# Third attention: the chain of its first half in quarters of 128 columns, with the PSUM banks dealt anew

## The chip, the core and the metric

The kernel runs on one core of a Trainium2 chip. A core has the tensor engine (PE, with its weight loads PEld), the vector engine (DVE), the scalar engine (ACT), GpSimd (POOL) and SyncE (SP), which here starts transfers. Each engine works off its own instructions in the order in which the program gives them, and waits only on semaphores. The metric is the device time of one execution in microseconds. The kernel before takes 116.27 us, the median of 3 runs (115.99 to 117.38).

## What is computed

A small vision tower on 16 images, each of 64 tokens with 64 features: patch embedding with layer norm, a windowed attention with two feed-forward nets, a second attention with a periodic bias, and a last block of a causal attention with 4 heads and a mixture of 8 gated experts, 2 of them for each token. The change lies in the last block, between its attention and its experts:

```python
x = h                                    # 1024 tokens x 64 features
q, k, v = rope(heads(rmsnorm(x)))        # 4 query heads, 2 key and value heads
scores = where(causal, q @ k.T / sqrt(16), -1e30)
y = softmax(scores) @ v                  # the third attention
x = x + y @ wo.T
flat = rmsnorm(x)                        # x * rsqrt(mean(x*x) + 1e-6) * ln2_w
probs = softmax(flat @ router_w.T)       # two best experts, weights that sum to 1
hh[e] = silu(flat @ w1[e].T) * (flat @ w3[e].T)
out = sum over e of weights[:, e] * (hh[e] @ w2[e].T)
result = layernorm(h + x + out)
```

## The kernel before

All activations lie in tiles of 128 partitions and 512 columns (COLS = 512). With tokens on the partitions, 512 columns are 8 blocks of 64 features. HC = 256 columns are one half (g = 0 or 1, four blocks), P = 128 columns a quarter (two blocks). PS is the PSUM, 8 banks of 512 columns of float32. The kernel writes the order of each engine out by hand and joins engines with named semaphores, so a step is late if anything ahead of it on its own engine is late. The tables of banks (TURNED_BANKS, UP_BANKS) say where products land.

The third attention works in four steps i = 0 to 3, two for each half g (i = 2g, 2g+1). For each step DVE takes the row maximum and subtracts it (shift3, L1217 and L1219), PE transposes (turn3, L589), ACT takes the exponential (probabilities3, L918), and PE multiplies by the values (mix3, L603). When both steps of a half are mixed, its chain follows:

- DVE divides by the row sum (divide: reciprocal L1228, product L1230),
- PE transposes back (mixed_to_features, L411), ACT copies out (attended_copy3, L922),
- PE opens a bank with the residual h4 in two float32r parts (open3, L613, which waits for POOL's split L1080 and L1082) and adds the output projection to it (output3, L618),
- ACT squares (squares3, L926), DVE sums (sum_squares3, L1392), POOL takes the power -0.5 (L1087),
- DVE scales the result twice, once rounded to float32r and once in full (high_part L1398, normalised L1374), and takes the difference (low_part, L1380),
- PE transposes both parts (parts_to_features, L626), and DVE and ACT copy one part each (turned_copy, L1385 and L937).

Then the expert products can begin: 22 chunks n = 0 to 21, the first 11 on half 0 and the others on half 1. A chunk is four float32r products of 512 columns on PE (L690, L691), a Silu on ACT (L956) and a product on DVE (L1437). The chain of half 1 runs between the first seven chunks: its output projection stands at n = 1, its transposes at n = 6. Its division and its transposes back (L411 again, bank 7) stand before chunk 0. stay_awake (L306) issues products of zeros that nobody reads.

On PE the order around the change is turn3(2), mixed_to_features(0), open3(0), output3(0), turn3(3), mix3(2), open3(1), mix3(3), stay_awake, parts_to_features(0), mixed_to_features(1), chunk 0. On DVE it is shift3(2), two scalings to h4 (L1168), divide(0), shift3(3), sum_squares3(0), high_part(0), normalised(0), low_part(0), divide(1), turned_copy(0), residual(0) (L1388), chunk 0.

Of the kernel before, what the change touches and what calls it, by code (L numbers as in the profile page):

```python
# [86 lines left out]
def build(nc, x0, x1, pack_a, pack_b, pack_c, pack_d, pack_e, out):  # L87
    with ExitStack() as ctx:
# [157 lines left out]

        def vo_part(h2, p, g):

            return vo[HALF * h2:HALF * h2 + HALF, p, 4 * g:4 * g + 4, :, h2, 0:HD]
# [47 lines left out]
        def _(pe):  # L297
# [109 lines left out]
            def mixed_to_features(name, bank, g):  # L407

                pe.wait_ge(sem(name + "_divided"), g + 1)
# [49 lines left out]
            mixed_to_features("att1", 0, 0)  # L459
# [12 lines left out]
            mixed_to_features("att1", 1, 1)  # L472
# [135 lines left out]
            def open3(g):  # L608


                pe.wait_ge(sem("h4_split"), 2 * (g + 1))
                for n in range(2):
                    mm(PS[:, 4 * g, 0:HC], ident_r[:, :], xf[:, g, n], start=(n == 0), stop=(n == 1), skip_group_check=True)  # L613

            def output3(g):
                pe.wait_ge(sem("att3_ready"), g + 1)
                for u in (2 * g, 2 * g + 1):
                    t = mm(PS[:, 4 * g, (u % 2) * P:(u % 2 + 1) * P], attended3[:, u * P:(u + 1) * P], c("fo"),  # L618
                           start=False, stop=True, skip_group_check=True)
                t.then_inc(sem("fo_mm"), 1)  # L620

            def parts_to_features(g):
                pe.wait_ge(sem("parts_ready"), g + 1)
                for s in range(2):
                    for u in (2 * g, 2 * g + 1):
                        t = tp(PS[:, TURNED_BANKS[s][g], (u % 2) * P:(u % 2 + 1) * P], parts[:, 2 * u + s].rearrange("q l d -> q (l d)"), ident)  # L626
# [37 lines left out]
            def half_ready(g):  # L664
                pe.wait_ge(sem("xf_ready0"), g + 1)
                pe.wait_ge(sem("xf_ready1"), g + 1)

            pe.wait_ge(sem("up_split"), 2)
            half_ready(0)
            for n in range(2 * CH):  # L670
                g, ch = n // CH, n % CH
                if n == 1:
                    output3(1)
                if n == 2:
                    pe.wait_ge(sem("h45_ready"), 1)
                if n == PARTS_AT:
                    pe.wait_ge(sem("h45_ready"), 2)
                    parts_to_features(1)
                if n == ROUTE_AT:
                    half_ready(1)  # L680
# [91 lines left out]
        def _(act):  # L772
# [147 lines left out]
            def attended_copy3(g):  # L920
                act.wait_ge(sem("att3_back"), g + 1)
                f(half(attended3, g), PS[:, 3 + 4 * g, 0:HC], ACT.Copy).then_inc(sem("att3_ready"), 1)  # L922

            def squares3(g):
                act.wait_ge(sem("fo_mm"), g + 1)
                f(squares_eps[:, 4 * g:4 * g + 4, 0:D], PS[:, 4 * g, 0:HC].rearrange("q (t d) -> q t d", d=D), ACT.Square,  # L926
                  scale=float(D) ** -0.5).then_inc(sem("rms2_squared"), 1)

            def high_part(g):

                act.wait_ge(sem("rms2_normed"), g + 1)
                f(parts[:, 4 * g:4 * g + 4, 0, :].bitcast(F32R), tiles(h5n)[:, 4 * g:4 * g + 4], ACT.Copy)\
                    .then_inc(sem("high_ready"), 1)

            def turned_copy(g):
                act.wait_ge(sem("parts_turned"), g + 1)
# [724 lines left out]
```

## Time and profile before

| | before |
|---|---|
| median of 3 runs | 116.27 us (115.99 to 117.38) |
| the profiled execution, its own time | 116.27 us |
| its span in the trace | 114.5 us |
| mean granted clock of the tensor engine | 0.989 |

```profile
span 114.5 us, 2195 instructions
...
PE 100.3 (88%) x825; PEld 65.2 (57%) x828; DVE 81.4 (71%) x173; ACT 64.0 (56%) x125; POOL 33.2 (29%) x68
...
PE   5998986899999998977699888899999999999720
...
DVE  0001515688979899889588984579589999986981
ACT  5003556776623853937378658467476667478040
POOL 7500017841840000000532083030012350869100
PEclk9999999999999999999999999999999999999995
...
PE 65%; DVE 20%; ACT 8%; issue 3%; POOL 1%; ACTq 0%; DVEq 0%; POOLq 0%
```

The first line is the span; the second gives busy time, share and instructions of each engine. The next five cut the span into 40 slices of 2.9 us, each digit the busy share in tenths, and PEclk the granted clock in tenths. The last line is the chain of work that ended last, shared out by engine. The third attention and its chain take slices 21 to 25, the expert products begin in the 26th. In the timeline below a row is start, duration, engine, line, operation, output<-inputs, and how often; a pair of brackets holds the idle time before it and who ended it. Rows of one kind that follow each other are merged, and their duration is then from the first start to the last end.

### The profile page before, as it was taken

The numbers are of one execution on the slowest core, as the hardware profiler recorded it, in microseconds if no ns is written. First come the engines' busy times: TensorE is split into PE (matmuls) and PEld (weight loads), VectorE is DVE, ScalarE is ACT, GpSimd is POOL, SyncE is SP. The second block draws the span as 40 slices with busy tenths as digits, with TensorE's granted clock in tenths as the row PEclk, the third lists the DMA queues.
The fourth block names the chain that finished last, engine by engine and source line by source line (L and its number), as shares of the span: only waits on it lengthen the run. The fifth ranks groups of instructions, "written<-read, shape, count | busy, mean of one in ns | idle before, by whom it ended". The sixth has DMA issues, their size and how long they took to land.

```text
span 114.5 us, 2195 instructions
## 1 busy us (share of the span) xinstructions
PE 100.3 (88%) x825; PEld 65.2 (57%) x828; DVE 81.4 (71%) x173; ACT 64.0 (56%) x125; POOL 33.2 (29%) x68
## 2 busy tenths in 40 slices
PE   5998986899999998977699888899999999999720
PEld 2344545567766765564378665687887884334400
DVE  0001515688979899889588984579589999986981
ACT  5003556776623853937378658467476667478040
POOL 7500017841840000000532083030012350869100
PEclk9999999999999999999999999999999999999995
DMA  3999993000000000000000000000000000000004
GB/s 109 399 397 416 445 407 136 0 0 0 0 6 0 0 3 6 3 0 0 0 0 6 0 0 6 0 0 0 0 0 6 3 0 0 3 0 0 0 0 92
DMA packets 2682, 6.99 MB, mean 61 GB/s; under 512 B 1264, under 2 KB 1392, under 8 KB 2544
## 3 DMA queue, kind: packets, MB, share of 16 engines
q1 hardware_dynamic: 2128, 6.72, 15.0%
q10 hardware_dynamic: 544, 0.13, 0.5%
q8 instruction: 6, 0.10, 0.4%
q14 instruction: 4, 0.03, 0.1%
HBM read 6.59 MB, written 0.26 MB: 60 GB/s over the span
## 4 chain that ended last, share of the span: by engine, by line
PE 65%; DVE 20%; ACT 8%; issue 3%; POOL 1%; ACTq 0%; DVEq 0%; POOLq 0%
PE PS L690 9%; PE PS L691 9%; PE PS L698 7%; PE PS L314 4%; PE PS L339 4%; PE PS L558 3%; PE PS L378 3%; PE PS L306 3%; PE PS L389 3%; ACT shared_f L791 3%; PE PS L349 3%; PE PS L403 3%; DVE shifted L1219 2%; DVE top L1217 2%; DVE sq_sums L1157 1%
## 5 line engine op out<-in xcount | busy, mean ns | idle before, releaser
L690 PE MATMUL PS<-xf,up_hi 128*128 128x512 f32 x44 | 17.8, 405 | 0.2 <-DVE xf L1385 0.2
L1437 DVE TENSOR_TENSOR shared_h<-PS,shared_f 128x512 f32<-128x512 f32 x22 | 15.0, 683 | 3.4 <-ACT shared_f L956 3.1
L691 PE MATMUL PS<-xf,up_lo 128*128 128x512 f32 x44 | 17.3, 394 | 0.0
L956 ACT ACTIVATE shared_f<-PS 128x512 f32<-128x512 f32 x22 | 13.1, 596 | 6.4 <-PE PS L691 6.2
L777 ACT ACT_TABLE_LOAD x9 | 11.5, 1283 | 0.9 <-PEq L1652 0.7
L1217 DVE TENSOR_REDUCE top<-PS 128x8 f32<-128x512 f32 x12 | 8.3, 688 | 2.5 <-PE PS L378 2.2
L690 PEld LDWEIGHTS PS<-xf,up_hi 128*128 128x128 f32 x44 | 8.3, 188 | 2.2 <-issue 0.4
L691 PEld LDWEIGHTS PS<-xf,up_lo 128*128 128x128 f32 x44 | 8.3, 188 | 1.8
L1219 DVE TENSOR_TENSOR shifted<-PS,top 128x512 f32<-128x512 f32 x12 | 8.3, 692 | 0.4
L852 ACT ACTIVATE probs<-PS 128x512 f32<-128x512 f32 x8 | 4.8, 597 | 5.9 <-PE PS L389 5.8
L791 ACT ACTIVATE shared_f<-PS,pack_b_sb 128x512 f32<-128x512 f32 x8 | 5.2, 684 | 4.9 <-PE PS L339 4.9
L698 PE MATMUL PS<-shared_h,down_w 128*64 128x512 f32 x32 | 7.7, 605 | 0.0
L314 PE MATMUL PS<-shared_x 128*64 128x256 f32 x48 | 7.1, 431 | 0.0
L1071 POOL TENSOR_SCALAR std<-sq_sums 128x8 f32<-128x8 f32 x1 | 0.2, 202 | 22.6 <-DVE sq_sums L1157 22.6
L306 PE MATMUL PS<-idle_bf 128*128 128x512 bf16 (+1 forms) x14 | 5.3, 492 | 1.5 <-POOL idle_bf L999 1.3
L1513 DVE TENSOR_TENSOR shared_x<-PS,up_w 128x512 f32<-128x512 f32 x8 | 5.2, 686 | 1.5 <-PE PS L698 1.1
L349 PE MATMUL PS<-shared_f,pack_b_sb 128*64 128x256 f32 x32 | 5.0, 405 | 1.0 <-ACT shared_f L791 0.9
L1235 DVE TENSOR_SCALAR pos_b<-pack_a_sb 128x64 f32<-128x64 f32 x1 | 0.3, 254 | 7.8 <-DMA pack_a_sb<-pack_a_dram 7.8
L1157 DVE TENSOR_REDUCE sq_sums<-squares 128x4 f32<-128x256 f32 x6 | 2.5, 418 | 4.6 <-ACT squares L800 4.4
L982 ACT ACTIVATE up_w<-PS 128x512 f32<-128x512 f32 x8 | 4.2, 599 | 2.7 <-PE PS L712 2.7
L378 PE MATMUL PS<-shared_h,q_groups 64*128 64x256 f32 x32 | 5.5, 422 | 0.0
L1125 POOL TENSOR_TENSOR shared_x<-shared_x 128x512 f32<-128x512 f32 x4 | 5.1, 1280 | 1.4 <-DVE shared_x L1513 1.3
(206 smaller groups left out, 210.1 us busy)
## 6 DMA issues: line engine op xcount, KB each, us to landing
shared_x<-x_dram SPq DMA_DIRECT2D x3, 576.0 KB, 4.6
shared_x<-x_dram SPq DMA_DIRECT2D x3, 512.0 KB, 7.2
up_w<-pack_d_dram SPq DMA_DIRECT2D x1, 1408.0 KB, 11.5
pack_c_sb<-pack_c_dram SPq DMA_DIRECT2D x1, 796.5 KB, 13.0
pack_b_sb<-pack_b_dram SPq DMA_DIRECT2D x1, 455.0 KB, 8.6
down_w<-pack_e_dram SPq DMA_DIRECT2D x1, 352.0 KB, 13.4
pack_a_sb<-pack_a_dram SPq DMA_DIRECT2D x1, 162.0 KB, 5.7
out_dram<-normed SPq DMA_DIRECT2D x2, 64.0 KB, 1.7
```

The costliest lines, as they stand in the source:

```text
L306: mm(PS[:, bank, 0:cols], idle_bf[:, 0:P], idle_bf[:, 0:cols], start=True, stop=True)
L314: m = mm(PS[HALF * s:HALF * s + HALF, 4 + g, 0:HC], x0_sb[:, n, PAIR + k * D:PAIR + (k + 1) * D], piece[:, n, (2 * k + s) * HC:(2 * k + s ...
L378: t = mm(PS[:, SCORE_BANKS[w % 2] + s, 0:HC], q_groups[r, w ^ s].rearrange("q h n -> q (h n)"), k_slots[r, w ^ s].rearrange("q h n -> q (h ...
L690: mm(up, up_hi[:, at:at + P], moving, start=True, stop=False)
L691: mm(up, up_lo[:, at:at + P], moving, start=False, stop=True).then_inc(sem("up_mm"), 1)
L698: t = mm(PS[HALF * s:HALF * s + HALF, bank, tok], down_w[:, DOWN_AT[ch]:DOWN_AT[ch] + D], hh[:, ch, s, tok], start=True, stop=True)
L777: f(table_use[:, :], const(1.0), func)
L791: f(hidden[:, m, :, g * HC:(g + 1) * HC], PS[:, u_banks[g]:u_banks[g] + 2, m * HC:(m + 1) * HC], ACT.Gelu_apprx_tanh, bias=b("ff1_b")[:, m ...
L956: f(gate[:, n % UPBUF, :], PS[:, UP_BANKS[n % UPBUF][0], :], ACT.Silu).then_inc(sem("gated"), 1)
L1217: v.reduce_max(tops, rows, AX).then_inc(sem(name + "_top"), 1)
L1219: v.tensor_tensor(shifted[:, n % 2, :].rearrange("q (b h n) -> q b h n", b=2, n=N), rows, tops.unsqueeze(3).to_broadcast([P, 2, 4, N]), AL ...
L1437: v.tensor_tensor(hh[:, ch, :, g * HC:(g + 1) * HC], PS[:, UP_BANKS[n % UPBUF][1], :].rearrange("q (s c) -> q s c", s=2), gate[:, n % UPBU ...
```

## The change

Half 0's chain, from the division to the copies, is done in two quarters u = 0, 1 of 128 columns, each in banks of its own; half 1 stays whole. Besides:

- The openings of the residual stand ahead of the transposes back. Quarter 0 is turned back into bank 4 and quarter 1 into bank 3 (BACK_BANKS); they are opened in banks 0 and 1 (H5_BANKS).
- shift3(3) is taken apart: its maximum stays behind the division, its subtraction stands behind both sums of squares.
- The transposes of the parts of quarter 0 stand ahead of mix3(3), those of quarter 1 behind it (banks 3, 2 and 5, 6, PARTS_BANKS). stay_awake is gone.
- All four copies of the transposed parts of half 0 are DVE's, and divide of half 1 stands behind them.
- ACT does both quarters' copies and squares ahead of probabilities3(2).
- POOL takes three powers, two of 128x2 and one of 128x4, in place of two of 128x4.

```diff
-        TURNED_BANKS = ((1, 4), (3, 7))
+        TURNED_BANKS = (4, 7)
+        BACK_BANKS = (4, 3)
+        H5_BANKS = (0, 1)
+        PARTS_BANKS = ((3, 2), (5, 6))
...
+            def quarter_to_features(u):
+                pe.wait_ge(sem("att3_divided"), u + 1)
+                tp(PS[:, BACK_BANKS[u], 0:P], quarter(s2, u), ident).then_inc(sem("att3_back"), 1)
...
+            def open3_quarters():
+                pe.wait_ge(sem("h4_split"), 2)
+                for u in range(2):
+                    for n in range(2):
+                        mm(PS[:, H5_BANKS[u], 0:P], ident_r[:, :], xf[:, 0, n, u * P:(u + 1) * P], start=(n == 0), stop=(n == 1), skip_group_check=True)
+
+            def output3_quarter(u):
+                pe.wait_ge(sem("att3_ready"), u + 1)
+                mm(PS[:, H5_BANKS[u], 0:P], quarter(attended3, u), c("fo"), start=False, stop=True, skip_group_check=True)\
+                    .then_inc(sem("fo_mm"), 1)
+
+            def quarter_parts_to_features(u):
+                pe.wait_ge(sem("parts_ready"), u + 1)
+                for s in range(2):
+                    t = tp(PS[:, PARTS_BANKS[u][s], 0:P], parts[:, 2 * u + s].rearrange("q l d -> q (l d)"), ident)
+                t.then_inc(sem("parts_turned"), 1)
...
             turn3(2)
-            mixed_to_features("att3", 3, 0)
-            open3(0)
-            output3(0)
+            open3_quarters()
+            quarter_to_features(0)
+            quarter_to_features(1)
+            output3_quarter(0)
+            output3_quarter(1)
             turn3(3)
             mix3(2)
-            open3(1)
+            open3_last()
+            quarter_parts_to_features(0)
             mix3(3)
-            stay_awake(2, 1)
-            parts_to_features(0)
-            mixed_to_features("att3", 7, 1)
+            quarter_parts_to_features(1)
+            mixed_to_features("att3", 7, 1, 3)
...
-            half_ready(0)
+            pe.wait_ge(sem("xf_ready0"), 4)
...
             values3(1)
+            attended_quarter(0)
+            attended_quarter(1)
+            squares3_quarter(0)
+            squares3_quarter(1)
             probabilities3(2)
-            attended_copy3(0)
-            squares3(0)
             probabilities3(3)
             bring_table(ACT.Silu)
-            turned_copy(0)
-            attended_copy3(1)
+            attended_last()
...
-            divide("att3", 3, 0, FH, FHD)
-            shift3(3)
+            divide3_quarter(0)
+            divide3_quarter(1)
+            highest("att3", rows3(3), 3)
             sum_squares3(0)
-            high_part(0)
-            normalised(0)
-            ve.wait_ge(sem("rms2_normed"), 1)
-            low_part(0)
-            divide("att3", 7, 1, FH, FHD)
-            turned_copy(0)
+            sum_squares3(1)
+            less_highest("att3", rows3(3), 3)
+            for u in range(2):
+                high_part(u)
+                normalised(u)
+                low_part(u)
+            quarter_copies(0)
+            quarter_copies(1)
+            divide3_last()
+            residual(1)
             residual(0)
```

The order on the tensor engine, from turn3(2) or what follows it to the first expert product. Before (L589 is turn3, L603 mix3, L411 the transposes back, L613 the openings, L618 the output projection, L626 the transposes of the parts):

```order
L589 MATMUL PS<-pack_a_sb,shifted 128x128 x4
L411 MATMUL PS<-pack_a_sb,s 128x128 x2
L613 MATMUL PS<-xf,ident_r 128x256 x2
L618 MATMUL PS<-pack_c_sb,attended 128x128 x2
L589 MATMUL PS<-pack_a_sb,shifted 128x128 x4
L603 MATMUL PS<-vo,probs 64x34 x8
L613 MATMUL PS<-xf,ident_r 128x256 x2
L603 MATMUL PS<-vo,probs 64x34 x8
L306 MATMUL PS<-idle_bf 128x512 x2
L626 MATMUL PS<-pack_a_sb,parts 128x128 x4
L411 MATMUL PS<-pack_a_sb,s 128x128 x2
L690 MATMUL PS<-xf,up_hi 128x512
```

In the changed program (L622 and L638 are the openings, L422 and L417 the transposes back, L626 the output projection, L599 turn3, L613 mix3, L632 the transposes of the parts, L718 the expert products):

```order
L622 MATMUL PS<-xf,ident_r 128x128 x4
L422 MATMUL PS<-pack_a_sb,s 128x128 x2
L626 MATMUL PS<-pack_c_sb,attended 128x128 x2
L599 MATMUL PS<-pack_a_sb,shifted 128x128 x4
L613 MATMUL PS<-vo,probs 64x34 x8
L638 MATMUL PS<-xf,ident_r 128x256 x2
L632 MATMUL PS<-pack_a_sb,parts 128x128 x2
L613 MATMUL PS<-vo,probs 64x34 x8
L632 MATMUL PS<-pack_a_sb,parts 128x128 x2
L417 MATMUL PS<-pack_a_sb,s 128x128 x2
L718 MATMUL PS<-xf,up_hi 128x512
L719 MATMUL PS<-xf,up_lo 128x512
```

The openings have moved ahead of the transposes back, and half of the parts' transposes ahead of the last mixing run. The transposes back of half 1 still stand directly ahead of the first expert product.

The order on the vector engine from the division of half 0 on, before (L1228 and L1230 are a division, L1217 and L1219 the maximum and its subtraction, L1385 the copy, L1388 the residual):

```order
L1228 RECIPROCAL r<-PS 128x4x4
L1230 TENSOR_TENSOR s<-PS,r 128x256
L1217 TENSOR_REDUCE top<-PS 128x8
L1219 TENSOR_TENSOR shifted<-PS,top 128x512
L1392 TENSOR_REDUCE sq_sums<-squares_eps 128x4
L1398 TENSOR_TENSOR parts<-PS,rstd_rms 128x4x64
L1374 TENSOR_TENSOR normed<-PS,rstd_rms 128x256
L1380 TENSOR_TENSOR parts<-normed,parts 128x4x64
L1228 RECIPROCAL r<-PS 128x4x4
L1230 TENSOR_TENSOR s<-PS,r 128x256
L1385 CAST xf<-PS 128x256
L1388 TENSOR_TENSOR attended<-PS,h 128x256
```

In the changed program, behind the two divisions by quarters (L1252 is the maximum, L1259 its subtraction, L1471 the sums, L1457 the copies, L1273 and L1275 the division of half 1):

```order
L1252 TENSOR_REDUCE top<-PS 128x8
L1471 TENSOR_REDUCE sq_sums<-squares_eps 128x2 x2
L1259 TENSOR_TENSOR shifted<-PS,top 128x512
L1435 TENSOR_TENSOR parts<-PS,rstd_rms 128x2x64
L1435 TENSOR_TENSOR normed<-PS,rstd_rms 128x128
L1451 TENSOR_TENSOR parts<-normed,parts 128x2x64
L1435 TENSOR_TENSOR parts<-PS,rstd_rms 128x2x64
L1435 TENSOR_TENSOR normed<-PS,rstd_rms 128x128
L1451 TENSOR_TENSOR parts<-normed,parts 128x2x64
L1457 CAST xf<-PS 128x128 x4
L1273 RECIPROCAL r<-PS 128x4x4
L1275 TENSOR_TENSOR s<-PS,r 128x256
```

The subtraction for step 3 has moved behind the sums of squares, and the division of half 1 behind the copies.

## Rows read from the trace of the kernel before

**Rows 1.** Busy time by stretches: window, us, PE, PEld, DVE, ACT, POOL, PEclk, DMA
```profile
66.20:73.10 6.90, 5.55 (x57) 3.87 (x59) 4.67 (x12) 4.21 (x10) 3.02 (x5) 1.00 0.01 2
73.10:93.90 20.80, 20.77 (x98) 17.02 (x99) 16.96 (x40) 13.64 (x26) 3.92 (x10) 1.00 0.01 1
```

**Rows 2.** Timeline of half 0's chain, from the mixing run to the output projection
```profile
64.76 1.42 PE L603 MATMUL PS<-vo,probs 128*64 128x34 f32 x32
...
66.23 0.26 DVE L1228 RECIPROCAL r<-PS 128x16 f32<-128x16 f32 x1
66.50 0.73 POOL L1082 TENSOR_TENSOR xf<-h,xf 128x256 fp32r<-128x256 f32 x1
66.52 0.42 DVE L1230 TENSOR_TENSOR s<-PS,r 128x256 f32<-128x256 f32 x1
...
67.00 0.44 PE L411 MATMUL PS<-pack_a_sb,s 128*128 128x128 f32 x2 [0.23 <-DVE s L1230]
...
67.28 0.30 PEld L613 LDWEIGHTS PS<-xf,ident_r 128*128 128x128 f32 x2
...
67.48 0.38 ACT L922 ACTIVATE attended<-PS 128x256 f32<-128x256 f32 x1
67.58 0.69 DVE L1219 TENSOR_TENSOR shifted<-PS,top 128x512 f32<-128x512 f32 x1
...
67.91 0.71 PE L618 MATMUL PS<-pack_c_sb,attended 128*128 128x128 f32 x4
```

**Rows 3.** Timeline further: the last mixing runs on PE, and the scaling
```profile
68.38 0.44 PEld L589 LDWEIGHTS PS<-pack_a_sb,shifted 128*128 128x128 f32 x4
...
68.66 0.38 ACT L926 ACTIVATE squares_eps<-PS 128x256 f32<-128x256 f32 x1 [0.80 <-PE PS L618]
68.99 0.55 PEld L603 LDWEIGHTS PS<-vo,probs 128*64 128x64 f32 x16 [0.17 <-issue]
...
69.08 0.42 DVE L1392 TENSOR_REDUCE sq_sums<-squares_eps 128x4 f32<-128x260 f32 x1 [0.81 <-ACT squares_eps L926]
...
69.58 0.30 PEld L613 LDWEIGHTS PS<-xf,ident_r 128*128 128x128 f32 x2
...
69.58 1.02 POOL L1087 TENSOR_TENSOR rstd_rms<-sq_sums,minus_half 128x4 f32<-128x4 f32 x1 [1.21 <-DVE sq_sums L1392]
...
70.02 0.55 PEld L603 LDWEIGHTS PS<-vo,probs 128*64 128x64 f32 x16
...
70.63 0.42 DVE L1398 TENSOR_TENSOR parts<-PS,rstd_rms 128x256 fp32r<-128x256 f32 x1 [1.13 <-POOL rstd_rms L1087]
...
70.97 0.41 DVE L1374 TENSOR_TENSOR normed<-PS,rstd_rms 128x256 f32<-128x256 f32 x1
```

**Rows 4.** Timeline of the end of the chain and the first expert products
```profile
72.53 0.20 PEld L411 LDWEIGHTS PS<-pack_a_sb,s 128*128 128x128 f32 x2 [0.20 <-DVE s L1230]
...
72.60 0.42 DVE L1385 CAST xf<-PS 128x256 fp32r<-128x256 f32 x1
...
73.13 0.47 PE L690 MATMUL PS<-xf,up_hi 128*128 128x512 f32 x1 [0.16 <-DVE xf L1385]
...
73.89 0.65 PEld L618 LDWEIGHTS PS<-pack_c_sb,attended 128*128 128x128 f32 x4
```

**Rows 5.** Groups by line and shape, of the nearest sizes
```profile
L911 ACT ACTIVATE vo<-PS 64x128 f32<-64x128 f32 x8 | 2.2, 275 | 0.3 <-PE PS L357 0.3
...
L1073 POOL TENSOR_TENSOR rstd<-std,minus_half 128x8 f32<-128x8 f32 x1 | 1.7, 1674 | 0.1
...
L1208 DVE COPY vo<-PS 64x128 f32<-64x128 f32 x4 | 1.1, 279 | 0.0
```

**Rows 6.** Busy time by stretches where PE waits, and after its last work
```profile
53.00:56.00 3.00, 1.86 (x14) 0.74 (x10) 2.46 (x10) 2.02 (x6) 0.35 (x2) 1.00 0.00 0
110.00:112.00 2.00, 0.00 (x0) 0.00 (x0) 1.78 (x7) 0.92 (x3) 0.00 (x0) 0.99 0.00 0
112.00:114.50 2.50, 0.00 (x0) 0.00 (x0) 0.17 (x1) 0.00 (x0) 0.00 (x0) 0.50 0.47 105
```

More of the change, by code:

```diff
@@ L245, in half, with quarter @@
             return t[:, g * HC:(g + 1) * HC]
+        def quarter(t, u):
+            return t[:, u * P:(u + 1) * P]
         def vo_part(h2, p, g):
@@ L471, in _ @@
             open_scores2(0)
-            mixed_to_features("att1", 1, 1)
+            mixed_to_features("att1", 1, 1, 2)
             ffn_up("ffn2", h2, (4, 2), 0)
@@ L619, in output3, with open3_last, output3_last @@
+            def open3_last():
+                pe.wait_ge(sem("h4_split"), 4)
+                for n in range(2):
+                    mm(PS[:, 4, 0:HC], ident_r[:, :], xf[:, 1, n], start=(n == 0), stop=(n == 1), skip_group_check=True)
+            def output3_last():
+                pe.wait_ge(sem("att3_ready"), 3)
+                for u in (2, 3):
+                    t = mm(PS[:, 4, (u % 2) * P:(u % 2 + 1) * P], quarter(attended3, u), c("fo"),
                            start=False, stop=True, skip_group_check=True)
@@ L929, in high_part, with attended_quarter @@
[L929 to L936, printed above, removed]
-                f(xf[:, g, 1, :], PS[:, TURNED_BANKS[1][g], 0:HC], ACT.Copy).then_inc(sem("xf_ready1"), 1)
+            def attended_quarter(u):
+                act.wait_ge(sem("att3_back"), u + 1)
+                f(quarter(attended3, u), PS[:, BACK_BANKS[u], 0:P], ACT.Copy).then_inc(sem("att3_ready"), 1)
@@ new lines, in squares3_quarter, with attended_last, squares3_last @@
+            def squares3_quarter(u):
+                act.wait_ge(sem("fo_mm"), u + 1)
+                f(squares_eps[:, 2 * u:2 * u + 2, 0:D], PS[:, H5_BANKS[u], 0:P].rearrange("q (t d) -> q t d", d=D), ACT.Square,
+                  scale=float(D) ** -0.5).then_inc(sem("rms2_squared"), 1)
+            def attended_last():
+                act.wait_ge(sem("att3_back"), 3)
+                f(half(attended3, 1), PS[:, 7, 0:HC], ACT.Copy).then_inc(sem("att3_ready"), 1)
+            def squares3_last():
+                act.wait_ge(sem("fo_mm"), 3)
+                f(squares_eps[:, 4:8, 0:D], PS[:, 4, 0:HC].rearrange("q (t d) -> q t d", d=D), ACT.Square,
+                  scale=float(D) ** -0.5).then_inc(sem("rms2_squared"), 1)
@@ new lines, in turned_copy_last, with residual, sum_squares3 @@
+            def turned_copy_last():
+                ve.wait_ge(sem("parts_turned"), 3)
+                v.tensor_copy(xf[:, 1, 0, :], PS[:, TURNED_BANKS[0], 0:HC]).then_inc(sem("xf_ready0"), 1)
+            def residual(n):
+                ts, bank, wide = H5_AT[n]
+                at = slice(ts.start * D, ts.stop * D)
+                v.tensor_tensor(h45[:, at], PS[:, bank, 0:wide], h4[:, at], ALU.add).then_inc(sem("h45_ready"), 1)
+            def sum_squares3(n):
+                ts = H5_AT[n][0]
+                ve.wait_ge(sem("rms2_squared"), n + 1)
+                v.reduce_sum(sq_sums[:, ts], squares_eps[:, ts], AX).then_inc(sem("rms2_sq_sum"), 1)
```

157 lines of the change are left out of this document (83 added, 74 removed).

## The prediction

> **What bounds the kernel now.** I read the busy time by stretches first. From 73.10 us to 93.90 us, while the expert products run, PE is busy 20.77 of 20.80 us; in the stretch before, from 66.20 to 73.10, it is busy 5.55 of 6.90 [rows 1]. So from the first expert product on PE sets the time, and in half 0's chain it waits. The reader is to take one thing from this: whatever moves the start of the first expert product, 73.13 us [rows 4], moves the end by as much, since nothing behind it has slack on PE. The later chain of half 1 hangs on that start too, by its place among the chunks. The prediction is therefore one number, the new start of that product.
>
> Then the timeline, link by link. The mixing run of half 0 ends at 64.76 + 1.42 = 66.18, the division runs 66.23 to 66.94, the two transposes back 67.00 to 67.44, ACT's copy starts at 67.48, the output projection at 67.91 and ends at 68.62 [rows 2]. Square, sum and power take 0.38, 0.42 and 1.02 us, and the first scaling starts at 70.63 [rows 3]. The copies start at 72.60 and the first expert product at 73.13 [rows 4]. A semaphore costs about 0.04 us from one engine to the next (67.44 to 67.48, [rows 2]), and 0.08 to POOL (69.50 to 69.58, [rows 3]). Two things beside the chain are hidden: the subtraction for step 3 (67.58, 0.69 us) lies under the copy and the projection [rows 2], and half 1's transposes back (72.53, a weight load of 0.20 us for both) under the wait for the copies [rows 4].
>
> **Prices of a quarter.** No row is a 128-column step of this chain. From below it is half of the 256-column one (0.21 us on DVE, 0.19 on ACT), from above the whole (0.42, 0.38). The nearest rows are 128 columns wide on 64 partitions: 0.279 us on DVE and 0.275 on ACT [rows 5]. I take 0.28 for both, so that two quarters take 0.56 of engine time where the half took 0.42. A power of 128x8 takes 1.67 us [rows 5] and one of 128x4 1.02 [rows 3], which is 0.16 us for a column, so 128x2 is estimated at 0.69; its bounds are 0.5 and 1.02. For a reciprocal of 128x8 I take 0.2, the one of 128x16 having 0.26 [rows 2]. Where the next instruction on DVE doesn't need the one before, it starts 0.08 us before that one's end (70.63 + 0.42 against 70.97, [rows 3]).
>
> **The front of the chain.** On DVE, quarter 0 is divided by 66.74 and quarter 1 by 67.2, against 66.94 for the half. But the openings now stand ahead of the transposes back, and they wait for POOL's split, 66.50 + 0.73 = 67.23, so they start at 67.28 as before [rows 2]. PE is held there with quarter 0 already divided. Four openings hold PE for about 0.45 us: four products of the projection take 0.71 us where two transposes take 0.44, or 0.11 to 0.14 for one more [rows 2], and two openings of twice the columns hold it 70.02 - 69.58 = 0.44 [rows 3], the upper bound being 0.88 for four. So the transposes back start at 67.73, 0.73 us later than now, and end at 68.17. The first is out a little earlier, and ACT's two copies run from 68.10 to 68.67 (two times 0.28, and one signal). Quarter 1's projection starts 0.05 later and takes 0.71 less two products, 0.49: 69.21. Its square follows to 69.53, its sum to 69.85. Before, the sum ended at 69.08 + 0.42 = 69.50 [rows 3].
>
> **What the subtraction does to PE.** The subtraction for step 3 now stands behind both sums. It starts at 69.77, 0.08 before the last sum's end, and takes 0.69 [rows 2]: 70.46, where it ended at 68.27. turn3(3) waits for it on PE, and behind turn3(3) everything else of PE is queued. The holding times come from the start of one weight load to that of the next: turn3 68.99 - 68.38 = 0.61, a mixing run 69.58 - 68.99 = 0.59, the openings of half 1 0.44 [rows 3]; two transposes of parts by the spacing above 0.22. From 70.50, PE reaches the parts of quarter 0 at 70.50 + 0.61 + 0.59 + 0.44 = 72.14 and those of quarter 1 at 72.14 + 0.22 + 0.59 = 72.95. The rest of the chain is ready long before. The first power is ready by 69.56 + 0.08 + 0.69 = 70.33, the second by 71.05. Quarter 1's scalings and difference, about 0.28 + 0.20 + 0.03 + 0.28 from 71.14, end at 71.95, a full 1.0 us before PE comes for them. So shorter steps and the powers no longer matter. Of probabilities3(2), which ACT now does behind the squares, the same holds: it needs 0.6 us from 69.53, and mix3(2) begins at 71.11.
>
> **The end of the chain.** Quarter 1's transposes run 72.95 to 73.39 (0.44, as the two of L411, [rows 2]). DVE copies it in two steps of 0.28, the second 0.08 early, from 73.43 to 73.91. Only now comes the division of half 1: reciprocal 0.26 from 73.83, product 0.42 [rows 2], with 0.03 between them: 74.54. The transposes back of half 1 stand ahead of the first expert product, so PE waits for it with the expert products queued behind. They start at 74.58 and hold PE some 0.25 us (0.20 for their loads, [rows 4]). The first expert product then starts at about 74.85. ACT's copy of half 1 (0.38) has until the first chunk is issued, 73.89 - 73.13 = 0.76 us [rows 4], and ends within about 0.6, so no further wait arises.
>
> **The sum.** 74.85 - 73.13 = +1.7 us. In parts: PE reaches the last parts and DVE has copied them by 73.91 instead of 73.02, +0.9; the division and transposes of half 1, which nothing covers any more, +0.8. The extra instructions elsewhere (the third power, the second residual of 0.28 on DVE) lie beside PE's work and cost nothing; the residual of quarter 1 would have to end by chunk 1, some 0.9 us later than chunk 0, and ends about 0.2 after the division. The profiled execution took 116.27 us with a span of 114.5, and is the median of the runs; 116.27 + 1.7 = 118.0 us. The terms that no row gives bound it so. If a quarter cost only half of its half, copies, squares and sums are 0.4 us shorter up to the subtraction, and the last copies 0.15: +1.15. If it cost the whole, 0.5 us and 0.25 are added, and openings of 0.88 would add 0.43: +2.6 at most with a part of that hidden.
>
> **Rivals.**
> *Pieces flow (faster).* PE isn't held: the back transposes are not kept behind the openings, and the last mixing run keeps nothing. Then quarter 1 is turned back by 67.6, projected by 68.4, summed by 69.05; its power is ready at 70.25 behind quarter 0's, its parts at 71.15, and turned and copied by 72.15. The first product would start at 72.2: -0.9, 115.4 us. For it speaks that each quarter's work is in banks of its own and that quarter 0 is divided 0.2 us sooner; against it that in the trace each group on PE starts behind the one written ahead of it, and that the openings and turn3(3) are written ahead. The place to decide is the last copy of half 0: it must end before 73.0. The Trainium skill (Perfetto Trace Analysis, Optimizing Scalar/DVE Operations) says that instructions broken up may let work finish sooner where ACT and DVE are not saturated but make other engines wait. By that rule the time would be this rival's 115.4 us; no run here shows it so far. The same skill (TensorE: Matmul & The Clock Gate, Step-by-step) says that only weight loads are pulled ahead and matmuls stay in program order, which speaks against it.
>
> *Only the first part.* The division of half 1 costs nothing on PE, the copies do: start at 74.0, +0.9, 117.2 us. It would need the transposes back to be ready by 73.9, while DVE has them behind the copies.
>
> *The clock falls.* PE would be idle about 1.2 us ahead of turn3(3) and again about 1 us ahead of the transposes of half 1, and the filling products of zeros are gone. The expert products are 0.23 us apart at the full level of 2.4 GHz (20.8 us hold 88 of them and the small ones, [rows 1]); at 1.2 GHz a chunk of four takes 0.9 us more. Two such chunks give +1.8 on top, 119.8 us. Against it: with PE busy 1.86 of 3.00 us the granted clock stayed at 1.00, and it stood at 0.99 in two microseconds with nothing on PE; only in the last 2.5 us of the trace did it fall to 0.50, which is the lower level [rows 6]. By the Trainium skill (TensorE: Matmul & The Clock Gate, What's actually happening) an idle array is what is throttled; the last row agrees with it.
>
> **Chances and range.** The forecast has 0.73, with a range of its own from 117.3 to 118.8 us. Only the first part 0.10; pieces flow, or cancel out, 0.05; the clock falls 0.05; another stall of 0.5 us or more 0.07. The range that leaves out about 2 in 10 reaches from the second rival, less the scatter of a median, to the upper bound: 116.9 to 118.9 us. Two per cent, about what a measurement of this kernel can tell from no change, is 2.3 us, so slower by over 2% is above 118.6 us. That takes the clock, the other stalls, and the upper tenth of the forecast: 0.22. Faster by over 2% would be under 113.9, more than the flowing pieces give: 0.02. Within 2%: 0.76.
>
> **What would show it.** In the profile after: the openings at 67.3 with the transposes back behind them; the subtraction for step 3 ending near 70.5 and PE idle for over 1 us until then; quarter 1's parts turned from about 72.95, a microsecond after their difference is ready; the transposes back of half 1 waiting for DVE's division until about 74.6; PE full from 74.85 on at a granted clock of 1.00. It is wrong if the first expert product starts before 73.5, or if the stretch of expert products is longer than 20.8 us.

## The result, and the profile after

The changed kernel takes 1.0194 times the time of the kernel before, 95% interval [1.0137, 1.0251]. On the 116.42 us of the kernel before (median of its 6 runs) that is 118.7 us; the forecast was 118.0. The ratio leaves out the four executions with the lowest clocks and rests on the other two, of 118.06 and 119.34 us. The median of all six is 121.31 us (118.06 to 123.41): the mean granted clock was 0.990 in the one of 118.06 us, and 0.973, 0.963, 0.952, 0.954 and 0.940 in the others. So two things are to be explained, a first expert product that starts later, as forecast, and a clock that falls in five of six executions, to which the prediction gave 0.05.

The profiled execution is the one of 123.41 us, with a mean clock of 0.940. From its page, the lines that answer to those shown of before:

```profile
span 121.6 us, 2210 instructions
...
PE 104.4 (86%) x826; PEld 68.6 (56%) x828; DVE 82.7 (68%) x183; ACT 63.7 (52%) x126; POOL 33.7 (28%) x69
...
PE   5968978999998998776999759699999999999820
...
PEclk9999999999999999999999955558999999999998
```

The span has grown by 7.1 us. The granted clock stands at half for four slices of 3.0 us each, from the third attention's last steps into the expert products. The timeline from the openings to the first expert product (same columns as in [rows 2]; L613 in the first row is the mixing run of half 0):

```profile
65.38 1.42 PE L613 MATMUL PS<-vo,probs 128*64 128x34 f32 x32
...
67.92 0.67 PE L622 MATMUL PS<-xf,ident_r 128*128 128x128 f32 x4 [0.53 <-POOL xf L1119]
...
68.42 0.41 PE L422 MATMUL PS<-pack_a_sb,s 128*128 128x128 f32 x2
...
70.00 0.72 DVE L1471 TENSOR_REDUCE sq_sums<-squares_eps 128x2 f32<-128x130 f32 x2 [1.58 <-ACT squares_eps L954]
...
70.63 0.68 DVE L1259 TENSOR_TENSOR shifted<-PS,top 128x512 f32<-128x512 f32 x1
...
71.46 1.09 PE L599 MATMUL PS<-pack_a_sb,shifted 128*128 128x128 f32 x4 [1.38 <-DVE shifted L1259]
...
72.47 0.29 DVE L1451 TENSOR_TENSOR parts<-normed,parts 128x128 f32<-128x128 f32 x1
...
75.64 0.69 PE L632 MATMUL PS<-pack_a_sb,parts 128*128 128x128 f32 x2
...
76.37 0.49 DVE L1457 CAST xf<-PS 128x128 fp32r<-128x128 f32 x2 [1.14 <-PE PS L632]
76.77 0.25 DVE L1273 RECIPROCAL r<-PS 128x16 f32<-128x16 f32 x1
77.05 0.42 DVE L1275 TENSOR_TENSOR s<-PS,r 128x256 f32<-128x256 f32 x1
...
77.53 0.29 PEld L417 LDWEIGHTS PS<-pack_a_sb,s 128*128 128x128 f32 x2 [1.60 <-DVE s L1275]
...
77.87 0.78 PE L718 MATMUL PS<-xf,up_hi 128*128 128x512 f32 x1
```

Each link of the forecast is in it. The openings wait for POOL's split and the transposes back stand behind them (67.92, 68.42). turn3(3) waits for DVE's late subtraction, with PE idle for 1.38 us (71.46). Quarter 1's parts are ready at 72.76 and are turned only at 75.64. The transposes back of half 1 wait for the division, 1.60 us between weight loads (77.53), and the first expert product stands behind them. To compare traces that start a little apart, I measure from the end of half 0's mixing run to the first expert product. Before it is 73.13 - 66.18 = 6.95 us [rows 2, 4]; forecast was 74.85 - 66.18 = 8.67; here it is 77.87 - 66.80 = 11.07. From the first expert product to the end there were 114.5 - 73.13 = 41.37 us before, and there are 121.6 - 77.87 = 43.73 now. The 7.1 us are 4.12 before that product, 2.36 behind it, and 0.62 by which this execution reached the mixing run later. The busy time by stretches shows why both are longer than the order makes them (columns as in [rows 1]):

```profile
68.00:69.00 1.00, 0.82 (x6) 0.58 (x6) 0.42 (x1) 0.25 (x2) 0.92 (x2) 1.00 0.00 0
69.00:70.00 1.00, 0.92 (x4) 0.70 (x4) 0.00 (x1) 0.48 (x3) 0.01 (x1) 0.68 0.00 0
70.00:70.50 0.50, 0.08 (x1) 0.00 (x0) 0.36 (x2) 0.39 (x2) 0.13 (x1) 0.50 0.00 0
...
82.00:83.00 1.00, 1.00 (x4) 0.81 (x3) 0.40 (x1) 0.27 (x1) 0.75 (x1) 0.50 0.00 0
83.00:84.00 1.00, 1.00 (x5) 0.80 (x5) 0.37 (x2) 0.60 (x1) 0.00 (x0) 0.99 0.00 0
```

The granted clock is 0.50, 1.2 GHz, from about 69.4 to 83 us, and only behind 83 do the expert products run at 2.4 GHz. turn3's four transposes take 1.09 us for 0.60 before, and the first product 0.78 for 0.47. The fall at 69.4 comes with PE busy 0.92 of that microsecond, ahead of the 1.38 us in which PE waits for the subtraction (70.08 to 71.46) and not behind them.

### The profile page after: what moved, and what is told of

It reads as the page before. It is cut to its first block, busy times and chain, and to the rows that moved or that the text cites. A ratio compares the mean times of both kernels' runs of the same rounds, so it can differ in the third digit from the quotient of the medians.

```text
span 121.6 us, 2210 instructions
## 1 busy us (share of the span) xinstructions
PE 104.4 (86%) x826; PEld 68.6 (56%) x828; DVE 82.7 (68%) x183; ACT 63.7 (52%) x126; POOL 33.7 (28%) x69
## 4 chain that ended last, share of the span: by engine, by line
PE 61%; DVE 20%; ACT 7%; DMA 5%; issue 3%; POOL 1%; SPq 1%; DVEq 0%; ACTq 0%
PE PS L718 9%; PE PS L719 9%; PE PS L726 6%; DMA shared_x<-x_dram 5%; PE PS L345 4%; DVE shifted L1259 3%; PE PS L568 3%; PE PS L384 3%; PE PS L395 3%; DVE top L1252 3%; ACT shared_f L819 3%; PE PS L355 3%; PE PS L409 2%; PE PS L320 2%; PE PS L613 2%
## 5 line engine op out<-in xcount | busy, mean ns | idle before, releaser
L718 PE MATMUL PS<-xf,up_hi 128*128 128x512 f32 x44 | 19.1, 435 | 0.0
L719 PE MATMUL PS<-xf,up_lo 128*128 128x512 f32 x44 | 18.4, 419 | 0.0
L718 PEld LDWEIGHTS PS<-xf,up_hi 128*128 128x128 f32 x44 | 9.1, 207 | 2.0
L719 PEld LDWEIGHTS PS<-xf,up_lo 128*128 128x128 f32 x44 | 9.0, 204 | 1.9
L1252 DVE TENSOR_REDUCE top<-PS 128x8 f32<-128x512 f32 x12 | 8.2, 687 | 2.1 <-PE PS L384 1.6
L1259 DVE TENSOR_TENSOR shifted<-PS,top 128x512 f32<-128x512 f32 x12 | 8.3, 691 | 0.9
L320 PE MATMUL PS<-shared_x 128*64 128x256 f32 x48 | 6.3, 391 | 1.2 <-DMA shared_x<-x_dram 1.2
L1123 POOL TENSOR_TENSOR rstd_rms<-sq_sums,minus_half 128x2 f32<-128x2 f32 (+1 forms) x3 | 2.4, 804 | 11.4 <-DVE sq_sums L1471 11.4
```

The lines of the kernel that those rows point to most:

```text
L320: m = mm(PS[HALF * s:HALF * s + HALF, 4 + g, 0:HC], x0_sb[:, n, PAIR + k * D:PAIR + (k + 1) * D], piece[:, n, (2 * k + s) * HC:(2 * k + s ...
L718: mm(up, up_hi[:, at:at + P], moving, start=True, stop=False)
L719: mm(up, up_lo[:, at:at + P], moving, start=False, stop=True).then_inc(sem("up_mm"), 1)
L1252: v.reduce_max(tops_of(n), rows, AX).then_inc(sem(name + "_top"), 1)
L1259: v.tensor_tensor(shifted[:, n % 2, :].rearrange("q (b h n) -> q b h n", b=2, n=N), rows, tops.unsqueeze(3).to_broadcast([P, 2, 4, N]), AL ...
```

## The experiments

Two theories are told apart. **Order:** three moves of steps (the openings ahead of the transposes back, the subtraction behind the sums, the division of half 1 behind the copies) cost 1.7 us together, the quarters themselves save a little. **Clock:** the waits that these moves put on PE let its clock fall, and products of zeros in the gaps (stay_awake) would keep it up. The rival to it is that low clocks are the chip's and have nothing to do with the kernel. Each experiment ran beside the kernel before on one chip, in three batches on three chips. Counts below are of executions with a mean granted clock under 0.98. A mean doesn't say where in the kernel the clock fell; only the trace of the profiled execution does.

**Each move alone, in the kernel before.** The first:

```diff
-            mixed_to_features("att3", 3, 0)
-            open3(0)
+            open3(0)
+            mixed_to_features("att3", 3, 0)
```

> The kernel before with one part of the change alone: the two openings of half 0 (L613) ahead of its transposes back (L411). The transposes then wait for POOL's split and the openings, 67.72 instead of 67.00 us, and the chain behind them has no slack before the first expert product: +0.7 us, 117.1 us. If the first part of the chain has slack, it stays at 116.4.

Measured: 1.0064 [1.0040, 1.0088], that is +0.75 us on 116.34. The term stands. One of ten executions had a low clock (0.941). It is the profiled one, and its trace has two falls:

```profile
37.00:39.00 2.00, 1.83 (x37) 1.52 (x36) 1.62 (x2) 1.59 (x3) 0.00 (x0) 1.00 0.00 0
39.00:41.00 2.00, 2.00 (x12) 1.48 (x8) 1.57 (x4) 0.92 (x3) 0.00 (x0) 0.55 0.00 0
...
69.00:70.00 1.00, 0.53 (x5) 0.37 (x4) 0.43 (x1) 0.38 (x1) 0.52 (x1) 0.96 0.00 0
70.00:71.00 1.00, 1.00 (x7) 1.00 (x6) 0.00 (x0) 0.34 (x1) 0.00 (x0) 0.50 0.06 16
```

The later one, at about 69.9 us, follows PE's waits of 0.50 us for POOL's split and 0.47 for ACT's copy. The earlier one, at about 39.2, lies in the second attention, which no edit touches, and PE was busy 1.83 of the 2.00 us ahead of it. So a fall needs no added gap, and the rival isn't ruled out by the count of low means alone.

The second:

```diff
...
-            shift3(3)
+            rows3 = PS[:, 5, :].rearrange("q (b h n) -> q b h n", b=2, n=N)
+            highest("att3", rows3, 3)
             sum_squares3(0)
+            less_highest("att3", rows3, 3)
```

> The kernel before with another part alone: the subtraction for step 3 behind the sum of squares of half 0. It ends at 70.1 us instead of 68.3, turn3(3) starts there, and PE's queue reaches the transposes of the parts at about 72.7 instead of 71.9: +0.8 us, 117.3 us. If PE's queue isn't what the parts wait for, it stays at 116.4. PE is idle for 1.5 us ahead of turn3(3), so by the clock's account some executions come out longer still, with a mean granted clock under 0.98.

Measured: 1.0315 [1.0286, 1.0345], 119.86 to 120.16 us, all four executions with clocks of 0.955 to 0.961. The time is 2.7 us above the 117.3 worked out for the order. In the trace, the rows of turn3(3) and of the clock behind it:

```profile
70.47 0.63 PE L589 MATMUL PS<-pack_a_sb,shifted 128*128 128x128 f32 x4 [1.62 <-DVE shifted L1221]
```

```profile
69.00:70.00 1.00, 0.00 (x0) 0.00 (x0) 0.70 (x2) 0.27 (x1) 0.19 (x1) 1.00 0.00 0
...
71.00:71.50 0.50, 0.50 (x17) 0.47 (x16) 0.50 (x2) 0.36 (x1) 0.00 (x0) 1.00 0.12 33
71.50:72.00 0.50, 0.50 (x10) 0.46 (x6) 0.47 (x2) 0.48 (x2) 0.00 (x0) 0.58 0.00 0
72.00:74.00 2.00, 2.00 (x20) 1.42 (x20) 0.57 (x3) 1.24 (x2) 0.00 (x0) 0.50 0.00 0
```

PE waits 1.62 us for the subtraction, goes on at full speed, and about 1 us later, busy again, is at half. So here the fall isn't seen in the gap itself but behind it. The same kernel with that gap filled:

```diff
             output3(0)
+            stay_awake(5, 6)
             turn3(3)
```

> The kernel before with the subtraction for step 3 behind the sum of squares, which took 120.0 us in every execution at a clock of 0.96, now with five products of zeros ahead of turn3(3). If the clock made 2.8 of its 3.6 us and the order 0.8, it takes 117.2 us at 0.99. If the order itself costs more than worked out, it stays above 118.5.

Measured: 117.23 us median, ratio 1.0046 [1.0012, 1.0081]. The nine timed executions take 116.47 to 118.96 us with clocks of 0.985 to 0.995, and 2.8 of the 3.6 us are gone, with more work on PE than before. That is the clearest pair: the same order, without and with five products of zeros, 120.0 and 117.2 us. The two ran on different chips, with the kernel before at 116.34 and 116.52 us beside them, and the profiled execution of the filled one took 190 us and is of no use here, so no trace shows the filled gap. The order costs +0.5 to +0.7 us, a little under the 0.8.

The third:

```diff
-            divide("att3", 7, 1, FH, FHD)
-            turned_copy(0)
+            turned_copy(0)
+            divide("att3", 7, 1, FH, FHD)
```

> The kernel before with a third part alone: the division of half 1 behind the copy of half 0 on DVE. The transposes back of half 1 stand ahead of the first expert product and wait until 73.7 us, which then starts at 73.95: +0.8 us, 117.3 us. If PE took the expert products past the waiting transposes, it would stay at 116.4.

Measured: 1.0120 [1.0075, 1.0164]; the three executions with a clock of 0.987 or more took 117.04, 117.30 and 117.42 us, +0.7 to +1.1, and the other four (0.962 to 0.979) up to 121.0. Its trace shows the wait and what follows it:

```profile
76.26 0.69 PE L411 MATMUL PS<-pack_a_sb,s 128*128 128x128 f32 x2 [1.14 <-DVE s L1230]
```

```profile
75.00:76.00 1.00, 0.12 (x2) 0.00 (x0) 0.81 (x3) 0.38 (x1) 0.00 (x0) 0.96 0.00 0
76.00:77.00 1.00, 0.74 (x3) 0.74 (x4) 0.54 (x2) 0.01 (x1) 0.00 (x0) 0.50 0.00 0
```

The expert products wait behind the transposes back, as forecast, and here the clock falls in that wait, at about 75.9. So falls are seen at either gap, behind the first and in the second. But the same execution has another one, at about 7.7 us, behind a wait of 1.81 us for the input, in a stretch that no edit touches, and it lowers the mean as much. The four low means are therefore not all the gap's.

**The kernel before without its fillers.**

```diff
             mix3(3)
-            stay_awake(2, 1)
             parts_to_features(0)
```

> The kernel before without its two products of zeros (stay_awake) ahead of the transposes of the parts. The order is unchanged. If these two fillers are what kept the clock up, some executions fall to 1.2 GHz and come out 2 to 7 us longer. If it is the longer wait of the changed order, this one stays at 116.3 us with a clock of 0.99.

Measured: 1.0004 [0.9979, 1.0029] where the clock stays, and four of ten executions with a low clock (0.843, 0.960, 0.976, 0.978) and up to 125.45 us. Beside it on the same chip the kernel before had none in 20 executions (0.983 to 0.997). The two products of zeros are worth nothing in the order, and the low clocks come when they go: four of ten against none of 20, which chance alone would give in under 1% of cases. The profiled execution (0.976) has its fall at about 73.1, behind the transposes of the parts, ahead of which PE had waited 1.23 us:

```profile
72.00:73.00 1.00, 0.86 (x6) 0.62 (x6) 0.84 (x4) 0.16 (x1) 0.00 (x0) 1.00 0.00 0
73.00:76.00 3.00, 2.84 (x11) 2.28 (x9) 1.07 (x3) 1.20 (x3) 0.00 (x0) 0.52 0.00 0
```

**The changed kernel with its gaps filled.** Both gaps:

```diff
             output3_quarter(1)
+            stay_awake(4, 6)
             turn3(3)
...
             quarter_parts_to_features(1)
+            pe.wait_ge(sem("xf_ready0"), 2)
+            stay_awake(4, 2)
             mixed_to_features("att3", 7, 1, 3)
```

> The changed kernel, with four products of zeros on PE ahead of turn3(3) (into bank 6) and four ahead of the transposes back of half 1 (into bank 2): in the two gaps in which PE waits for DVE. Nothing else moves. If the order costs 1.7 us and the fallen clock the rest, the fillers leave the order's part alone: 1.7 us over the kernel before, 118.1 us, with a granted clock of 0.99 in every execution and executions within 1 us of each other. If the low clock is a disturbance that has nothing to do with the gaps, the executions stay at 118 to 123 us with mean clocks down to 0.94.

Measured: 118.44, 118.35 and 117.69 us in the timed executions, clocks of 0.988 to 0.994, ratio 1.0166 [1.0120, 1.0212] on 116.47 us, so +1.9 us. The profiled execution took 520 us; nothing is drawn from it, and no trace shows the filled gaps. Then one gap each:

```diff
             output3_quarter(1)
+            stay_awake(4, 6)
             turn3(3)
```

> The changed kernel with four products of zeros in the first gap alone, ahead of turn3(3). If that gap alone lets the clock fall, every execution comes out at 118.1 to 118.5 us with a mean granted clock of 0.98 or more. If the second gap, ahead of the transposes back of half 1, lets it fall too, some executions have a clock under 0.98 and take 119 to 121 us, with the fall only at the first expert products.

Measured: 120.76, 120.12 and 118.13 us at 0.962, 0.978 and 0.995. Two of three still fall, as the account with two gaps had it. The profiled execution took 236 us, and nothing is drawn from it either, so where the clock fell isn't known. Three executions are few, and this is the weakest result here: beside it, on that chip, the kernel before itself had 3 of 14 low (0.979, 0.848, 0.57).

```diff
             quarter_parts_to_features(1)
+            pe.wait_ge(sem("xf_ready0"), 2)
+            stay_awake(4, 2)
             mixed_to_features("att3", 7, 1, 3)
```

> The changed kernel with four products of zeros in the second gap alone, ahead of the transposes back of half 1. If the first gap is what lets the clock fall, most executions stay as those of the changed kernel, 119 to 123 us with mean clocks of 0.94 to 0.975. If it is the second, they come out at 118.1 to 118.5.

Measured: 120.96, 121.05 and 120.91 us at 0.958 to 0.959, 118.80 at 0.973, and 118.25 and 117.84 at 0.987 and 0.990. Four of six low, with only the gap ahead of turn3(3) left open (and the same chip's 3 of 14 beside them). In the trace that gap is passed at full clock, and the fall comes behind it, at about 71.7:

```profile
70.99 0.63 PE L599 MATMUL PS<-pack_a_sb,shifted 128*128 128x128 f32 x4 [1.38 <-DVE shifted L1261]
```

```profile
70.00:71.00 1.00, 0.01 (x1) 0.04 (x1) 1.00 (x4) 0.41 (x1) 0.90 (x2) 1.00 0.00 0
71.00:72.00 1.00, 1.00 (x14) 0.83 (x16) 0.96 (x5) 0.34 (x1) 0.48 (x1) 0.83 0.00 0
```

turn3(3) starts at 70.99, with the mixing run's end at 66.63: 4.36 us, where the prediction had 70.50 - 66.18 = 4.32. Up to there its working is confirmed at full clock.

**The moves taken back in the changed kernel,** with fillers in both gaps (not shown in the diffs): two ahead of turn3(3) throughout, and ahead of the transposes back four, then two, two and at last one. First the subtraction alone:

```diff
             highest("att3", rows3(3), 3)
+            less_highest("att3", rows3(3), 3)
             sum_squares3(0)
             sum_squares3(1)
-            less_highest("att3", rows3(3), 3)
```

> The changed kernel with the subtraction for step 3 directly behind its maximum and fillers in both gaps; the division of half 1 stays behind the copies. By the prediction's working the first expert product starts at 73.95 us, 0.9 us earlier than in the changed kernel: 117.2 us. Compared with the kernel that has the division early too (117.1), the division would be worth 0.4 us. If the division is the whole of what is left, 117.5 us.

Measured: 117.31 us median, 1.0098 [1.0065, 1.0131], all five clocks 0.984 or more. Forecast by the working was 117.2. What is left in its trace is the division's wait:

```profile
65.79 0.41 PE L613 MATMUL PS<-vo,probs 128*64 128x34 f32 x8
...
72.73 0.49 DVE L1460 CAST xf<-PS 128x128 fp32r<-128x128 f32 x2 [0.37 <-PE PS L632]
73.14 0.25 DVE L1276 RECIPROCAL r<-PS 128x16 f32<-128x16 f32 x1
73.42 0.42 DVE L1278 TENSOR_TENSOR s<-PS,r 128x256 f32<-128x256 f32 x1
...
73.90 0.44 PE L417 MATMUL PS<-pack_a_sb,s 128*128 128x128 f32 x2 [0.34 <-DVE s L1278]
74.09 0.48 PE L721 MATMUL PS<-xf,up_hi 128*128 128x512 f32 x1
```

The copies are done at 73.22 and the expert products start at 74.09, 0.87 us later, with the division and the transposes back between: the +0.8 of the prediction. From the mixing run's end at 66.20 it is 7.89 us, against 73.95 - 66.18 = 7.77 worked out.

The division forward too, between the copies:

```diff
             quarter_copies(0)
-            quarter_copies(1)
             divide3_last()
+            quarter_copies(1)
```

> The changed kernel with the subtraction for step 3 directly behind its maximum, the division of half 1 between the copies of quarter 0 and those of quarter 1, and two fillers in each gap. By the working of the prediction the first expert product starts at 73.5 us instead of 74.85, that is 0.4 us over the kernel before: 116.8 us. If the order of these two steps is not what costs, it stays at 118 us.

Measured: 117.13 us median, 1.0076 [1.0049, 1.0103]; one of five low (0.957). Between the end of the mixing run and the first expert product lie 7.43 us (66.76 to 74.19), worked out 73.5 - 66.18 = 7.32. It is 0.46 less than with the subtraction alone, but as times the two are not told apart (1.0076 and 1.0098).

The transposes back ahead of the openings as well, so that of the change only the quarters are left and what came with them: all four copies on DVE, quarter 0's parts turned ahead of mix3(3), ACT's copies and squares ahead of probabilities3(2), and the fillers in new places:

```diff
-            open3_quarters()
             quarter_to_features(0)
             quarter_to_features(1)
+            open3_quarters()
```

> As the kernel with the subtraction and the division moved forward, and besides the transposes back of both quarters ahead of the openings, as before the change. The quarters alone are left of the change. By the working of the prediction the first expert product starts at 72.7 us, 0.4 us earlier than in the kernel before: 116.0 us. If splitting in quarters costs more in instructions than it gives, it is no faster than the one with the openings first, 116.8 us.

Measured: 116.40 us median, 1.0003 [0.9978, 1.0028]. The rows that matter (L613 the mixing run, L1460 the last copies, L721 the first expert product):

```profile
65.82 0.66 PE L613 MATMUL PS<-vo,probs 128*64 128x34 f32 x16
...
72.59 0.48 DVE L1460 CAST xf<-PS 128x128 fp32r<-128x128 f32 x2
...
73.22 0.47 PE L721 MATMUL PS<-xf,up_hi 128*128 128x512 f32 x1
```

That is 6.74 us, 0.21 under the 6.95 of before, where 0.4 was worked out; in the time it can't be seen. No run takes the quarters apart from what came with them, so the 0.21 is all of it together.

At last three of the four copies on ACT, one on DVE (quarter_copies then makes one copy; its loop and the semaphores are left out of the diff):

```diff
-            quarter_copies(0)
             divide3_last()
             quarter_copies(1)
...
             bring_table(ACT.Silu)
+            for u, s in ((0, 0), (0, 1), (1, 1)):
+                act.wait_ge(sem("parts_turned"), u + 1)
+                f(xf[:, 0, s, u * P:(u + 1) * P], PS[:, PARTS_BANKS[u][s], 0:P], ACT.Copy).then_inc(sem("xf_ready1"), 1)
             attended_last()
```

> The changed kernel with the quarters alone (subtraction and division early, transposes back ahead of the openings, fillers in the two gaps), and besides three of the four copies of half 0 on ACT, which is idle there, one on DVE. DVE then divides half 1 as soon as its mixing run ends, and only one copy follows: the first expert product starts at about 72.6 us of the timeline before, 0.5 us earlier than in the kernel before: 115.9 us. If DVE's copies are not what the first expert product waits for, it stays with the kernel before, 116.4.

Measured: 116.20 us median of 12, 0.9992 [0.9968, 1.0016], all clocks 0.980 or more.

```profile
65.89 0.66 PE L613 MATMUL PS<-vo,probs 128*64 128x34 f32 x16
...
72.66 0.28 DVE L1464 CAST xf<-PS 128x128 fp32r<-128x128 f32 x1
...
73.05 0.47 PE L722 MATMUL PS<-xf,up_hi 128*128 128x512 f32 x1
```

6.50 us to the first expert product, worked out 6.4, and 0.45 less than before. The 115.9 us forecast lie just outside the interval, which begins at 116.0 and holds no change. This is the best version, and it isn't shown to beat the kernel before.

| kernel | mixing run's end to first expert product, us | worked out | ratio |
|---|---|---|---|
| before | 6.95 | | 1 |
| changed | 11.07 (clock fallen) | 8.67 | 1.0194 |
| subtraction early, filled | 7.89 | 7.77 | 1.0098 |
| and division early | 7.43 | 7.3 | 1.0076 |
| and transposes back first | 6.74 | 6.5 | 1.0003 |
| and copies on ACT | 6.50 | 6.4 | 0.9992 |

The changed kernel with its gaps filled and nothing moved has no usable trace, so its row is missing; its time is 1.0166.

## Why the prediction was right, and where it was wrong

**What bounds it.** Right. PE is full from the first expert product on, and the start of that product passes through to the end: 41.37 us lie behind it before, 41.4 (114.4 - 73.05) with the copies shared. In the profiled execution of the changed kernel 43.73 do; the products at half the clock from 77.87 to 83 account for the 2.36 more (half of 5.1 us is 2.6). By that the prediction's own second sign of being wrong, a longer stretch of expert products, came true: from the start of the first to that of the last they take 22.6 us before (73.1 to 95.7) and 24.9 after (77.9 to 102.8). Its remark that 20.8 us hold all 88 of them is a misreading for the same reason; the spacing of 0.23 us is right.

**The price of a quarter.** Right. A step of 128 columns took 0.28 to 0.29 us on DVE (72.47, 0.29, in the timeline after) where 0.28 was taken, the powers 1.38 us for two where 2 x 0.69 was estimated, the reciprocal 0.21 for 0.2. Only the pairs on ACT were taken too long: its two copies together took 0.45 us, not 0.56.

**The front, +0.7 at the transposes back.** Right: alone it costs +0.75 us.

**The subtraction.** Right in place and nearly in size. turn3(3) starts 4.36 us behind the mixing run for 4.32 forecast; alone and with its gap filled it costs 0.5 to 0.7 us for the 0.8 expected. Taken back in the changed kernel it brings 118.35 to 117.31 (both filled, on two chips and with two fillers fewer), 1.0 us for 0.9.

**The division of half 1.** Right: 0.87 us between the copies and the expert products, 0.8 forecast; alone +0.7 to +1.1.

**The sum.** +1.7. The undisturbed executions of the changed kernel and of its filled forms took 118.06, 117.69, 118.35, 118.44, 118.13, 118.25 and 117.84 us, that is +1.2 to +2.0 on the 116.4 to 116.5 of the kernel before beside them. The changed kernel itself has one such execution, the 118.06 us. Alone, the three moves cost 0.75, 0.5 to 0.7 and 0.7 to 1.1 us, 2.0 to 2.5 in all; with the 0.2 of the quarters off, that is at the upper end of what they cost together.

**The clock.** Wrong, and this is the step that failed: the sentence "Against it: with PE busy 1.86 of 3.00 us the granted clock stayed at 1.00", from which the rival got 0.05. Five of six executions have it. Those rows showed one execution of one kernel with its fillers in place, and [rows 6] showed that such a stretch can be passed, not that it always is. The prediction named the two gaps and the fillers that were gone, and gave them next to no weight. What the runs put in its place: the same order with and without products of zeros at 117.2 and 120.0 us, on two chips (nine of nine, and none of four executions at a clock over 0.98); the kernel before without its two fillers low in four of ten, with them in none of the 20 beside it; the changed kernel low in five of six, with both gaps filled in none of three, and with moves taken back besides in one of 32. The price, "two such chunks" or 1.8 us on top, 119.8 in all, is near two of the low executions (119.34 and 120.50) and 2.3 to 3.6 us short of the other three. What it left out is that the chain ahead of the expert products runs at half speed as well when the fall comes early, 11.07 us for 8.67.

So the range holds for the ratio, 118.7 us, while the median of the six executions, 121.3, lies above it. The forecast of the order, 118.0, is met by the one execution at full clock, 118.06; that the ratio comes within 0.7 us of it is partly luck, since half of what it rests on is the 119.34 us with a clock of 0.973. The rule of the Trainium skill that speaks for such a change (Perfetto Trace Analysis, Optimizing Scalar/DVE Operations: broken-up instructions may let work finish sooner when ACT and DVE aren't saturated) holds only weakly here: with the moves taken back, the quarters and what came with them brought the first expert product 0.21 us forward, and the time not measurably. The Trainium skill's other statement, that matmuls keep their order (TensorE: Matmul & The Clock Gate, Step-by-step), the traces bear out, the division's wait above all: with the late division PE waits 1.14 us at the transposes back, with the expert products behind them.

**What stays open.** Why one execution in six keeps the clock, and which wait lets it fall in the changed kernel. In its profiled execution the clock fell at 69.4 us, behind the wait of 0.53 us for POOL and ahead of the 1.38 us before turn3(3); with the second gap filled it fell at about 71.7, behind that wait; with the openings alone moved, at about 69.9. So the early openings may make a gap of their own, which no filler was put into. With a single gap filled too few executions were timed to say how much each gap adds, and on that chip the kernel before was low in 3 of 14 too. So there are low clocks that have nothing to do with these gaps, as the falls at 7.7 and 39.2 us in untouched stretches show. They are hardly the whole: in the two batches in which the kernel before had no low clock in 45 executions, its variants without the fillers, with the late subtraction and with the late division had them in four of ten, four of four and four of seven. That the gaps make falls more frequent is thus shown by counts, with four located falls beside them; what decides a single execution is not shown.

## What to carry to other kernels

In a program whose engines run hand-written orders, look first at what stands behind a step that is moved back: here a subtraction and a division that had been hidden each held PE's queue, and splitting the chain in quarters, the headline of the change, was worth at most 0.2 us, beside the 0.75, 0.5 to 0.7 and 0.7 to 1.1 us that the three moves cost. Measure the products of zeros before taking them out; with them gone, or with a wait added in front of dense products, look at the clock of every execution, not at one. And if a profile shows the clock up, that is one execution's answer.

## What the runs showed of the hardware

- The granted clock fell to half not only while PE waited (75.9 us with the late division) but up to about 1 us behind a wait, with PE busy again (turn3(3) at 70.47 at full clock, 0.58 in 71.5 to 72.0), and once with PE busy 1.83 of the 2.00 us before (39.2 us with the openings alone moved). It stayed there while the expert products kept PE full, for the last 5.1 of 13.6 us in the profiled execution (69.4 to 83.0) and for 3 to 7 us in all in the others shown. The Trainium skill (TensorE: Matmul & The Clock Gate, What's actually happening) has the array throttled when idle and let go by activity; the falls at the gaps agree with the direction, the one at 39.2 us doesn't.
- With products of zeros in bfloat16 that nobody reads in the gap, the clock stayed up in nine of nine executions and 2.8 us were gone, with five of them; without, in none of four, on another chip.
- How often and how far the clock falls differs by kernel: 119.86 to 120.16 us in four of four for one, 115.93 to 125.45 for another with the same order as the kernel before.
